# A layer-normalised attention and gate layer: x of batches 1 to 3 arrives with features on partitions, and only token factors are turned

## The chip, the cores and the metric

The kernel runs on one core of one Trainium2 chip. The metric is the device time of one execution in microseconds (us). Beside it stands one profiled execution, whose trace gives every instruction of the five engines: TensorE (PE), VectorE (DVE), ScalarE (ACT), GpSimd (POOL) and SyncE (SP), which here issues nearly all transfers.

## The reference, cut to what matters

For four batches of 512 tokens with 1024 features, in float32:

```
xn = (x - mean(x)) / sqrt(var(x) + 1e-5)          # per token, over features
q, k, v = xn @ Wq.T, xn @ Wk.T, xn @ Wv.T         # 32 query heads, 8 key/value heads, 128 wide
q, k = rmsnorm(q) * q_norm_w, rmsnorm(k) * k_norm_w
attn = softmax(q k^T / sqrt(128) + slope * (key - query), causal)
s = (attn @ v) @ Wo.T
g = silu(xn @ W.T + bias + low-rank part)
out = x + s * g
```

## The kernel before, in words

Every float32 product on TensorE is made of three products of halves: an operand is split into a high part (ACT rounds it) and a low part (the rest, by DVE or POOL), and `three` (L507) multiplies high by high, low by high and high by low.

The work is 32 groups (4 batches by 8 key/value heads), and each group `n` has four steps `j` = 0 to 3, one for each query head of the group. A step is written `(g, j)` here, with `g` the group inside its batch. In every step PE makes the scores of this head and the weighted values of the head before, turns some rows, then makes the projections of the **next** group in two or four "pieces" (`unit_pieces`; 12 products of 448 columns each), then four output products c = 0 to 3 of the head two steps back, with the turning of the probabilities between them. The projection of a group is a 2 x 2 block scheme with seven products P1 to P7: P1, P2 in steps with j = 0, P6, P7 with j = 1, P4 with j = 2, P5, P3 with j = 3. Three of them use blocks of x as they are, four use sums of blocks, made by POOL (`x_sum`).

The engines share no scheduler: the order on each engine is the order in which its block of code issues it (`step` of each engine), and semaphores do the rest. Two PSUM banks hold the pieces and the output products in turn, so output product c = 0 needs the bank of the first piece's row block, c = 1 the second's, c = 2 the bank that DVE frees by adding c = 0 (`add_out`, L1344), and c = 3 the one that it frees by adding c = 1. The turned probabilities use three banks, and the fourth turning needs the first's, which DVE frees (`probs_lo`).

The normalised x of a batch is prepared in the last three groups of the batch before. x lies with tokens on partitions (`xtok`): DVE takes statistics (`ln_stats`, L1241), ACT scales the rows (`ln_scale`, L911), PE turns it in 14 "fills" of four 128 x 128 transposes each (`turn_x`, L581) at steps (6, 3), (7, 0) and (7, 1), and for each fill ACT takes the high part out of PSUM (`x_hi`, L858) and DVE the low part (`x_lo`, L1284). A piece of the next batch waits for the fills of its block.

POOL's order in a step: the position bias of the next head (`bias_of`, L1100), the low part of an output weight (`low_b`, L1092), the low part of v when j = 0 (`values_lo`, L1105), then the low parts of two or four weight tiles (`low_product`, L1081), for the pieces of the next step; they run at the end of a step and in the first 7.7 us of the next one.

## Time and profile before

| what | value |
| --- | --- |
| time, median of 3 runs | 2654.61 us (2654.4 to 2656.84) |
| the profiled execution | 2655.72 us, of which the span of its instructions is 2653.9 us |
| PE busy | 2583.1 us, 97% of the span |
| DVE, ACT, POOL busy | 1699.8, 1764.6, 1718.0 us (64, 66, 65%) |
| mean granted TensorE clock | 0.995 of full speed |
| DMA | 414.78 MB, 156 GB/s in the mean |

A busy PE is counted by instructions that overlap, so its share doesn't show small waits. How long a step takes is read from the timeline: from the first score product of a step (128 x 128) to that of the next. The differences between steps of the same `j` are what a batch's preparation costs.

### The profile page before, as it was taken

How to read it: one execution, taken by the hardware profiler on the slowest of the kernel's cores; microseconds unless marked ns; L12 is line 12 of the kernel's file. 1: busy time of each engine (PE TensorE's matmuls, PEld its weight loads, DVE VectorE, ACT ScalarE, POOL GpSimd, SP SyncE). 2: the span in 40 equal slices, each digit the busy share in tenths (PEclk: the TensorE clock that was granted, in tenths of full speed). 3: DMA queues.
4: the chain of work that ended last, by engine and by line, in shares of the span. 5: the costliest groups of instructions: out<-in, count | busy, mean ns of one | idle time of the engine just before them, and what ended most of it. 6: DMA issues, size and time to landing. Idle time of an engine off the chain costs nothing.

```text
span 2653.9 us, 39893 instructions
## 1 busy us (share of the span) xinstructions
PE 2583.1 (97%) x13840; PEld 2288.9 (86%) x13840; DVE 1699.8 (64%) x3533; ACT 1764.6 (66%) x4633; POOL 1718.0 (65%) x839
## 2 busy tenths in 40 slices
PE   6789999999999999999999999999999999999997
PEld 5778888888888888888888888888888888888886
DVE  7565656666766665666667666666666756656656
ACT  4565666767767666667766667666777666667764
POOL 3577887785767565655667756565666766656555
PEclk9899999999999999999999999999999999999999
DMA  7868878875354333433344433433334533333323
GB/s 283 289 219 278 265 261 272 271 258 166 118 171 154 113 106 118 140 112 118 106 137 155 128 119 111 144 106 118 109 104 137 189 106 108 115 116 112 112 78 131
DMA packets 171896, 414.78 MB, mean 156 GB/s; under 512 B 31024, under 2 KB 63920, under 8 KB 170800
## 3 DMA queue, kind: packets, MB, share of 16 engines
q1 hardware_dynamic: 170144, 410.19, 47.1%
q8 instruction: 112, 1.84, 0.3%
q10 hardware_dynamic: 1552, 2.04, 0.2%
q14 instruction: 88, 0.72, 0.1%
HBM read 339.81 MB, written 89.13 MB: 162 GB/s over the span
## 4 chain that ended last, share of the span: by engine, by line
PE 90%; DVE 3%; DMA 2%; POOL 2%; ACT 1%; SPq 1%; issue 0%; ACTq 0%; POOLq 0%; DVEq 0%
PE proj L508 21%; PE proj L510 21%; PE proj L509 21%; PE tr L608 5%; PE tr L588 3%; PE sc L508 3%; PE sc L509 3%; PE sc L510 3%; PE ot L509 3%; PE ot L510 3%; PE ot L508 3%; DMA wu<-xtok 1%; PE tr L581 1%; DMA wl<-wu 1%; POOL wl L1081 1%
## 5 line engine op out<-in xcount | busy, mean ns | idle before, releaser
L1081 POOL TENSOR_TENSOR wl<-wl,wh 128x896 fp32r<-128x896 f32 x428 | 909.1, 2156 | 552.3 <-ACT wh L788 552.2
L508 PE MATMUL proj<-wh,xh 128*128 128x448 f32 x1792 | 670.7, 374 | 7.3 <-ACT raw L827 2.2
L509 PE MATMUL proj<-wl,xh 128*128 128x448 f32 x1792 | 657.9, 367 | 0.0
L510 PE MATMUL proj<-wh,xl 128*128 128x448 f32 x1792 | 657.8, 367 | 0.0
L1092 POOL TENSOR_TENSOR wb_lo<-wb_lo,wb_hi 128x1024 fp32r<-128x1024 f32 x128 | 307.7, 2404 | 303.7 <-ACT wb_hi L822 303.7
L879 ACT ACTIVATE misc<-misc,negmax 128x128 f32<-128x128 f32 (+3 forms) x512 | 286.7, 565 | 266.3 <-DVE negmax L1319 266.1
L508 PE MATMUL proj<-o_hi,wb_hi 128*128 128x512 f32 x1024 | 425.2, 415 | 7.4 <-DVE acc L1344 3.5
L1344 DVE TENSOR_TENSOR acc<-acc,proj 128x512 f32<-128x512 f32 x476 | 324.8, 683 | 149.7 <-PE proj L510 147.8
L858 ACT ACTIVATE pT_hi<-tr 128x512 fp32r<-128x512 f32 (+3 forms) x512 | 197.5, 440 | 325.9 <-PE tr L608 325.9
L510 PE MATMUL proj<-o_hi,wb_lo 128*128 128x512 f32 x1024 | 403.6, 394 | 0.0
L509 PE MATMUL proj<-o_lo,wb_hi 128*128 128x512 f32 x1024 | 401.3, 392 | 0.0
L788 ACT ACTIVATE wh<-wl 128x896 fp32r<-128x896 f32 x428 | 387.9, 965 | 19.7 <-DMA wl<-wu 19.2
L1314 DVE TENSOR_TENSOR raw<-raw,proj 128x448 f32<-128x448 f32 x320 | 197.4, 617 | 301.9 <-PE proj L510 300.1
L508 PEld LDWEIGHTS proj<-wh,xh 128*128 128x128 f32 x1792 | 337.9, 189 | 37.1 <-ACT raw L827 4.9
L510 PEld LDWEIGHTS proj<-wh,xl 128*128 128x128 f32 x1792 | 337.4, 188 | 30.0
L509 PEld LDWEIGHTS proj<-wl,xh 128*128 128x128 f32 x1792 | 338.1, 189 | 27.8
L1319 DVE CUSTOM_DVE_ANT_0 misc<-sc,misc 128x128 f32<-128x128 f32 (+3 forms) x512 | 240.9, 487 | 175.9 <-PE sc L510 174.7
L1284 DVE TENSOR_TENSOR pT_lo<-tr,pT_hi 128x512 fp32r<-128x512 f32 (+3 forms) x512 | 226.6, 484 | 74.7 <-ACT pT_hi L858 74.4
L834 ACT ACTIVATE junk<-raw 128x128 f32<-128x128 f32 x640 | 189.8, 301 | 97.2 <-DVE raw L1314 93.4
L886 ACT ACTIVATE misc<-misc,rs_inv 128x128 f32<-128x128 f32 (+3 forms) x512 | 245.2, 558 | 1.0 <-DVE rs_inv L1325 1.0
L508 PEld LDWEIGHTS proj<-o_hi,wb_hi 128*128 128x128 f32 x1024 | 193.4, 189 | 51.7 <-DVE acc L1344 4.1
L1100 POOL TENSOR_SCALAR misc<-misc,slope 128x512 f32<-128x512 f32 x128 | 233.6, 1825 | 4.1 <-DMA misc<-rel 4.1
(135 smaller groups left out, 4438.1 us busy)
## 6 DMA issues: line engine op xcount, KB each, us to landing
...
wb_lo<-wo_in SPq DMA_DIRECT2D x128, 512.0 KB, 3.3
...
```

The costliest lines, as they stand in the source:

```text
L508: pe.matmul(out, hi_l, hi_r, start=first, stop=False, skip_group_check=onto)
L509: pe.matmul(out, hi_l, lo_r, start=False, stop=False, skip_group_check=onto)
L510: return pe.matmul(out, lo_l, hi_r, start=False, stop=last, skip_group_check=onto)
L788: act.activation(w_slot(wh, w), w_slot(wl, w, True), ACT.Copy).then_inc(w_hi_done, 1)
L879: act.activation(p, p, ACT.Exp, bias=negmax[:, i:i + 1], scale=-1.0, accum_out=rowsum[:, i:i + 1]).then_inc(exp_done, 1)
L886: ins = act.activation(p, p, ACT.Copy, scale=rs_inv[:, i:i + 1])
L1081: pool.tensor_tensor(w_slot(wl, w), w_slot(wl, w, True), w_slot(wh, w), ALU.subtract).then_inc(w_ready, 1)
L1092: pool.tensor_tensor(wb_lo[:, v % 2, :], wb_lo[:, v % 2, :].bitcast(F32), wb_hi[:, v % 2, :], ALU.subtract).then_inc(wb_ready, 1)
L1100: pool.tensor_scalar(bias_sb[:, m % 2, :], rel_sb[:], slope[:, m % H:m % H + 1], None, ALU.mult).then_inc(bias_ready, 1)
L1284: dve.tensor_tensor(dst, bank, hi, ALU.subtract).then_inc(tr_free, 1)
L1319: dve.tensor_tensor_reduce(prob[:, P_AT[i]:P_AT[i] + w], sc_ps[i % 2][:, 0:w], bias_sb[:, m % 2, S - w:S], -1.0, 3e38, ALU.add, ALU.min, n ...
L1344: dve.tensor_tensor(a, a, bank, ALU.add).then_inc(out_free, 1)
```

## The change

For batches 1 to 3 x is loaded into the same place with features on partitions (eight chunks of 128 features, 512 tokens along each row). Its values then need a factor and a shift that vary along the row, the same for every partition. They come from the tokens: each quarter of x with tokens on partitions is loaded a second time into a new buffer `rows` at steps (4, 3), (5, 0), (5, 1), (5, 2) (`load_rows`), DVE takes its statistics (`row_stats`), ACT and DVE form factor and shift at (5, 3), DVE spreads each over 128 columns (`spread_rows`), PE turns the two (`turn_tokens`, eight transposes at step (6, 0)) and DVE copies them back (`take_rows`). DVE multiplies four parts of x by the factor at (6, 1) (`x_mul`), POOL adds the shift (`x_add`) behind its weight tiles of (6, 1) and ahead of those of (6, 2). ACT and DVE then split each of the seven blocks in one instruction each, of 1024 elements per partition, out of SBUF (`x_hi_later`, `x_lo_later`).

The position bias has one buffer in place of two, so POOL makes the next head's bias only when all four score tiles of this head have been read, and the buffer `junk` of ACT's squares is smaller, with a semaphore on every square.

```diff
+    at = {(6, 3): (P1, P2), (7, 0): (P7, P4, None, P6), (7, 1): (None, None, P5, P3)}
+    return [(b + 1, p) if p is not None else None for p in at.get((g, j), ())]
+
+
+def x_tile(n, j):
+
+    b, g = divmod(n, HKV)
+    t = {(4, 3): 0, (5, 0): 1, (5, 1): 2, (5, 2): 3}.get((g, j))
+    return None if t is None or b + 1 == BATCH else (b + 1, t)
+
+
+def x_count(b, p):
+
+    return NP * (b - 1) + [P1, P2, P7, P4, P6, P5, P3].index(p) + 1
...
+            if (n % HKV, j) == (6, 0) and n + HKV < NG:
+                keys += [("r", n // HKV + 1, i) for i in range(2)]
+            keys += [("p", 4 * n + j, k) for k in range(NT)]
...
-        misc = sb("misc", [P, PW + 5 * S])
-        prob, bias_sb = misc[:, 0:PW], misc[:, PW:PW + 2 * S].rearrange("p (a n) -> p a n", a=2)
-        z_buf, e_buf, rel_sb = (misc[:, PW + i * S:PW + i * S + S] for i in (2, 3, 4))
+        misc = sb("misc", [P, PW + 6 * S])
+        prob = misc[:, 0:PW]
+        bias_sb, z_buf, e_buf, rel_sb = (misc[:, PW + i * S:PW + i * S + S] for i in range(4))
+
+        rows = misc[:, PW + 4 * S:PW + 6 * S]
...
+        def x_part(i):
+
+            chunk, at = i % 2 * 4, i // 2 * 256
+            part = flat(xtok).rearrange("p (k n) -> p k n", k=NK)[:, chunk:chunk + 4, at:at + 256]
+            return part, slice(at, at + 256)
...
-                sp.dma_start(xtok[:], x_tok[b - 1]).then_inc(x_in, 16)
+                chunks = xT[b * NK:b * NK + NK].rearrange("k p n -> p k n")
+                sp.dma_start(flat(xtok).rearrange("p (k n) -> p k n", k=NK), chunks).then_inc(x_in, 16)
+
+            def load_rows(b, t):
+
+                if t > 0:
+                    sp.wait_ge(row_stat, NT * (b - 1) + t)
+                elif b > 1:
+                    sp.wait_ge(x_norm, 4 * (b - 1))
+                sp.dma_start(rows, x_tok[b - 1][:, t, :]).then_inc(rows_in, 16)
...
+            def turn_tokens(b, i):
+
+                key = ("r", b, i)
+                pe.wait_ge(row_spread, b)
+                bank = turn_bank(key)
+                for t in range(NT):
+                    at = i * S + t * P
+                    mm = pe.transpose(bank[:, t * P:t * P + P], rows[:, at:at + P], ident_sb[:])
...
-                for u in pieces:
+                for i, u in enumerate(unit_pieces(n, j)):
                     piece(*u)
-                    if fills:
-                        turn_x(fills.pop(0))
+                    if (n % HKV, j) == (6, 0) and n + HKV < NG and i < 2:
+                        turn_tokens(n // HKV + 1, i)
                 if n + 1 == NG and v % 2 == 0:
                     out_first(v)
                 elif v >= 0:
                     out_ready(v)
                     for c in range(2):
                         out_proj(v, c)
-                        if fills:
-                            turn_x(fills.pop(0))
...
+            def x_hi_later(b, p):
+
+                if p in FILL_SUM:
+                    act.wait_ge(sum_ready, 4 * b + FILL_SUM[p])
+                else:
+                    act.wait_ge(x_norm, 4 * (b - 1) + {P1: 1, P2: 2, P4: 4}[p])
+                act.wait_ge(u_done, u_count(HKV * b - 1, p, 1))
+                act.activation(xh[:, p], x_block(p), ACT.Copy).then_inc(x_hi_done, 1)
...
-                if m >= 2:
-                    wait_alone(pool, scored, 4 * m - 4)
-                pool.tensor_scalar(bias_sb[:, m % 2, :], rel_sb[:], slope[:, m % H:m % H + 1], None,
+                if m >= 1:
+                    wait_alone(pool, scored, 4 * m)
+                pool.tensor_scalar(bias_sb[:], rel_sb[:], slope[:, m % H:m % H + 1], None,
...
+            def split_of(b, p, f):
+
+                if b == 0:
+                    pool.wait_ge(tr_done, TR["x", 0, f] + 1)
+                else:
+                    pool.wait_ge(x_ready, x_count(b, p))
+
+            def x_add(b, i):
+
+                part, at = x_part(i)
+                pool.wait_ge(x_mul_done, 4 * (b - 1) + i + 1)
+                pool.wait_ge(row_free, 2 * b)
+                shift = rows[:, S + at.start:S + at.stop].unsqueeze(1).to_broadcast([P, 4, 256])
+                pool.tensor_tensor(part, part, shift, ALU.add).then_inc(x_norm, 1)
...
-                if (g, j) == (6, 3) and next_x is not None and b > 0:
+                if j == 0 and n + 1 < NG:
+                    values_lo(n)
+                if (g, j) == (7, 1) and next_x is not None:
+                    x_sum(next_x, P5)
+                    x_sum(next_x, P3)
+                if (g, j) == (6, 2) and next_x is not None:
+                    x_add(next_x, 2)
+                    x_add(next_x, 3)
+                if (g, j) == (6, 3) and next_x is not None:
                     x_sum(next_x, P7)
                 if (g, j) == (7, 0) and next_x is not None:
                     x_sum(next_x, P6)
-                if j == 0 and n + 1 < NG:
-                    values_lo(n)
-                if (g, j) == (7, 0) and next_x is not None:
-                    x_sum(next_x, P5)
-                    x_sum(next_x, P3)
...
+                if (g, j) == (6, 1) and next_x is not None:
+                    x_add(next_x, 0)
+                    x_add(next_x, 1)
...
+            def spread_rows(b):
+
+                dve.wait_ge(ln_newton, 5 * (b + 1))
+                for i, column in enumerate((rinv_x, shift_x)):
+                    place = rows[:, i * S:i * S + S].rearrange("p (t n) -> p t n", t=NT)
+                    ins = dve.tensor_copy(place, column[:].unsqueeze(2).to_broadcast([P, NT, P]))
+                ins.then_inc(row_spread, 1)
+
+            def take_rows(b, i):
+                dve.wait_ge(tr_done, TR["r", b, i] + 1)
+                dve.tensor_copy(rows[:, i * S:i * S + S], tr_ps[TR["r", b, i] % 3][:]).then_inc(row_free, 1)
+
+            def x_mul(b, i):
+
+                part, at = x_part(i)
+                dve.wait_ge(x_in, 16 * b)
+                dve.wait_ge(row_free, 2 * b - 1)
+                factor = rows[:, at].unsqueeze(1).to_broadcast([P, 4, 256])
+                dve.tensor_tensor(part, part, factor, ALU.mult).then_inc(x_mul_done, 1)
+
+            def x_lo_later(b, p):
+                dve.wait_ge(x_hi_done, x_count(b, p))
+                dve.tensor_tensor(xl[:, p], x_block(p), xh[:, p], ALU.subtract).then_inc(x_ready, 1)
...
+                        x_lo_later(*turned.pop(0))
+                    fill = fills.pop(0) if fills else None
+                    if fill:
+                        turned.append(fill)
+                    if (g, j) == (6, 0) and next_x and i < 2:
+                        take_rows(b + 1, i)
                     if (j, p, t) == (0, P2, 0):
                         gate_sum(n)
-                    if j == 1 and g == ln_group(b + 1) and next_x:
-                        ln_stats(b + 1, (i,))
+                    if (g, j) == (6, 1) and next_x:
+                        x_mul(b + 1, i)
...
-                turned += fills
+                if x_tile(n, j):
+                    row_stats(*x_tile(n, j))
                 if turned:
-                    x_lo(turned.pop(0))
+                    x_lo_later(*turned.pop(0))
                 add_out(v, 0)
-                if turned:
-                    x_lo(turned.pop(0))
                 if j == 2 and more:
                     row_factors(n + 1, 0)
-                if j == 2 and g == ln_group(b + 1) and next_x:
+                if (g, j) == (5, 3) and next_x:
                     ln_factors(b + 1)
+                    spread_rows(b + 1)
                 add_out(v, 1)
-                if turned:
-                    x_lo(turned.pop(0))
                 for k in range(3):
                     probs_lo(m, k)
                 if j == 1:

```

What moves is shown on POOL, where it makes and consumes x. First POOL before, from the weight tiles of step (6, 1) to those of (6, 3), for batch 2; `wl` is the low part of a weight tile, `misc<-misc,slope` the bias, L1115 the block sum for P7.

```order
L1081 TENSOR_TENSOR wl<-wl,wh 128x896 x4
L1100 TENSOR_SCALAR misc<-misc,slope 128x512
L1092 TENSOR_TENSOR wb_lo<-wb_lo,wb_hi 128x1024
L1081 TENSOR_TENSOR wl<-wl,wh 128x896 x2
L1100 TENSOR_SCALAR misc<-misc,slope 128x512
L1092 TENSOR_TENSOR wb_lo<-wb_lo,wb_hi 128x1024
L1115 TENSOR_TENSOR xtok<-xtok 128x2x512
L1081 TENSOR_TENSOR wl<-wl,wh 128x896 x4
```

The same stretch of POOL now, where L1125 is the weight tile, L1144 the bias, L1136 `low_b`, L1190 `x_add` and L1164 the block sum for P7:

```order
L1125 TENSOR_TENSOR wl<-wl,wh 128x896 x4
L1190 TENSOR_TENSOR xtok<-xtok,misc 128x4x256 x2
L1144 TENSOR_SCALAR misc<-misc,slope 128x512
L1136 TENSOR_TENSOR wb_lo<-wb_lo,wb_hi 128x1024
L1190 TENSOR_TENSOR xtok<-xtok,misc 128x4x256 x2
L1125 TENSOR_TENSOR wl<-wl,wh 128x896 x2
L1144 TENSOR_SCALAR misc<-misc,slope 128x512
L1136 TENSOR_TENSOR wb_lo<-wb_lo,wb_hi 128x1024
L1164 TENSOR_TENSOR xtok<-xtok 128x4x256
L1125 TENSOR_TENSOR wl<-wl,wh 128x896 x4
```

Four additions of 1024 elements stand in POOL's row now, two ahead of a bias and two ahead of the weight tiles of P3.

The second place is DVE in step (7, 0), from the scaling of two query heads to the addition of the output products. Before:

```order
L1274 SCALAR_TENSOR_TENSOR raw<-raw,tmp 128x4x128 x2
L1284 TENSOR_TENSOR xl<-tr,xh 128x512 x2
L1348 TENSOR_SCALAR misc<-misc 128x512
L1284 TENSOR_TENSOR xl<-tr,xh 128x512 x2
L1344 TENSOR_TENSOR acc<-acc,proj 128x512
L1284 TENSOR_TENSOR xl<-tr,xh 128x512
L1344 TENSOR_TENSOR acc<-acc,proj 128x512
L1284 TENSOR_TENSOR xl<-tr,xh 128x512
```

And now (L1376 the scaling, L1352 `x_lo_later`, L1450 the gate's sum, L1446 `add_out`):

```order
L1376 SCALAR_TENSOR_TENSOR raw<-raw,tmp 128x4x128 x2
L1352 TENSOR_TENSOR xl<-xtok,xh 128x1024 x2
L1450 TENSOR_SCALAR misc<-misc 128x512
L1352 TENSOR_TENSOR xl<-xtok,xh 128x1024
L1446 TENSOR_TENSOR acc<-acc,proj 128x512 x2
```

Six low parts out of PSUM have become three out of SBUF, of twice the size, and the third of them (block P6) stands ahead of the addition of output product c = 0.

The third place is POOL in step (7, 0) and (7, 1). Before, `low_b`, the sum for P6, `values_lo`, the sums for P5 and P3:

```order
L1092 TENSOR_TENSOR wb_lo<-wb_lo,wb_hi 128x1024
L1119 TENSOR_TENSOR xtok<-xtok 128x2x512
L1105 TENSOR_TENSOR v_lo<-raw,v_hi 128x512
L1123 TENSOR_TENSOR xtok<-xtok 128x2x512
L1126 TENSOR_TENSOR xtok<-xtok 128x2x512
L1081 TENSOR_TENSOR wl<-wl,wh 128x896 x4
L1100 TENSOR_SCALAR misc<-misc,slope 128x512
L1092 TENSOR_TENSOR wb_lo<-wb_lo,wb_hi 128x1024
```

And now (L1149 `values_lo`, L1168 the sum for P6, L1172 and L1175 those for P5 and P3):

```order
L1136 TENSOR_TENSOR wb_lo<-wb_lo,wb_hi 128x1024
L1149 TENSOR_TENSOR v_lo<-raw,v_hi 128x512
L1168 TENSOR_TENSOR xtok<-xtok 128x4x256
L1125 TENSOR_TENSOR wl<-wl,wh 128x896 x4
L1144 TENSOR_SCALAR misc<-misc,slope 128x512
L1136 TENSOR_TENSOR wb_lo<-wb_lo,wb_hi 128x1024
L1172 TENSOR_TENSOR xtok<-xtok 128x4x256
L1175 TENSOR_TENSOR xtok<-xtok 128x4x256
```

The sum for P6 has moved behind `values_lo`, and those for P5 and P3 to the step after.

## Rows read from the trace of the kernel before

**Rows 1.** The page: the chain that ended last, share of the span by engine.

```profile
PE 90%; DVE 3%; DMA 2%; POOL 2%; ACT 1%; SPq 1%; issue 0%; ACTq 0%; POOLq 0%; DVEq 0%
```

**Rows 2.** Timeline, PE: start us, us; the first score product of a step.

```profile
582.68 0.22 PE L508 MATMUL sc<-kT_hi,qT_hi 128*128 128x128 f32 x1
...
749.81 0.22 PE L508 MATMUL sc<-kT_hi,qT_hi 128*128 128x128 f32 x1
...
1065.15 0.22 PE L508 MATMUL sc<-kT_hi,qT_hi 128*128 128x128 f32 x1
...
1086.33 0.22 PE L508 MATMUL sc<-kT_hi,qT_hi 128*128 128x128 f32 x1
...
1107.51 0.22 PE L508 MATMUL sc<-kT_hi,qT_hi 128*128 128x128 f32 x1
...
1122.79 0.22 PE L508 MATMUL sc<-kT_hi,qT_hi 128*128 128x128 f32 x1
...
1143.96 0.22 PE L508 MATMUL sc<-kT_hi,qT_hi 128*128 128x128 f32 x1
...
1186.32 0.22 PE L508 MATMUL sc<-kT_hi,qT_hi 128*128 128x128 f32 x1
...
1202.24 0.22 PE L508 MATMUL sc<-kT_hi,qT_hi 128*128 128x128 f32 x1
...
1281.06 0.22 PE L508 MATMUL sc<-kT_hi,qT_hi 128*128 128x128 f32 x1
...
1304.04 0.22 PE L508 MATMUL sc<-kT_hi,qT_hi 128*128 128x128 f32 x1
...
1328.69 0.22 PE L508 MATMUL sc<-kT_hi,qT_hi 128*128 128x128 f32 x1
...
1351.56 0.22 PE L508 MATMUL sc<-kT_hi,qT_hi 128*128 128x128 f32 x1
...
1388.02 0.22 PE L508 MATMUL sc<-kT_hi,qT_hi 128*128 128x128 f32 x1
```

**Rows 3.** Timeline, PE, in step (7, 0) of batch 1: one turning of x.

```profile
1311.16 0.60 PE L581 MATMUL tr<-ident_sb,xtok 128*128 128x128 f32 x4
...
1311.51 0.45 PE L508 MATMUL proj<-wh,xh 128*128 128x448 f32 x1
```

**Rows 4.** Timeline, DVE and POOL, at the start of a step with j = 3.

```profile
1124.18 2.89 DVE L1274 SCALAR_TENSOR_TENSOR raw<-raw,tmp 128x512 f32<-128x512 f32 x2
...
1121.72 4.20 POOL L1081 TENSOR_TENSOR wl<-wl,wh 128x896 fp32r<-128x896 f32 x2 [2.55 <-ACT wh L788]
...
1125.90 2.53 POOL L1100 TENSOR_SCALAR misc<-misc,slope 128x512 f32<-128x512 f32 x1
```

**Rows 5.** Groups by form: xcount | busy us, mean ns | idle before, releaser.

```profile
L1092 POOL TENSOR_TENSOR wb_lo<-wb_lo,wb_hi 128x1024 fp32r<-128x1024 f32 x128 | 307.7, 2404 | 303.7 <-ACT wb_hi L822 303.7
...
L1241 DVE BATCH_NORM_STATS2 bn<-xtok 128x6 f32<-128x512 f32 x32 | 20.5, 682 | 7.1 <-DMA xtok<-x_first 7.1
...
L1274 DVE SCALAR_TENSOR_TENSOR raw<-raw,tmp 128x512 f32<-128x512 f32 x160 | 154.6, 998 | 1.1
...
L822 ACT ACTIVATE wb_hi<-wb_lo 128x1024 fp32r<-128x1024 f32 x128 | 134.6, 1052 | 9.5 <-DMA wb_lo<-wo_in 9.5
...
L1366 DVE TENSOR_TENSOR xtok<-xtok,acc 128x512 f32<-128x512 f32 x28 | 38.4, 1372 | 0.1
...
L1284 DVE TENSOR_TENSOR xl<-tr,xh 128x512 fp32r<-128x512 f32 x56 | 37.8, 683 | 18.7 <-ACT xh L858 18.4
...
L1392 DVE TENSOR_TENSOR acc<-acc 128x896 f32<-128x896 f32 x2 | 2.2, 1083 | 0.0
```

**Rows 6.** Timeline, POOL, PE and DVE, late in step (4, 0) of batch 1.

```profile
1079.40 1.29 POOL L1105 TENSOR_TENSOR v_lo<-raw,v_hi 128x512 fp32r<-128x512 f32 x1
...
1083.38 0.48 PE L508 MATMUL proj<-o_hi,wb_hi 128*128 128x512 f32 x1
...
1081.31 0.69 DVE L1344 TENSOR_TENSOR acc<-acc,proj 128x512 f32<-128x512 f32 x1 [1.41 <-PE proj L510]
```

More of the change, by code:

```diff
@@ L110 @@
 TR = {key: i for i, key in enumerate(TURNS)}
-LO = {key: i for i, key in enumerate(k for k in TURNS if k[0] != "z")}
+LO = {key: i for i, key in enumerate(k for k in TURNS if k[0] not in "zr")}
 PROJS = proj_order()
@@ L1244, in ln_stats, with row_stats, ln_variance @@
                 ins.then_inc(ln_stat, 1)
-                wait_alone(dve, ln_stat, 2 * b + 1)
+                wait_alone(dve, ln_stat, 1)
+                ln_variance(0)
+            def row_stats(b, t):
+                dve.wait_ge(rows_in, 16 * (NT * (b - 1) + t + 1))
+                for i in range(2):
+                    ins = dve.bn_stats(bn[:, t, 6 * i:6 * i + 6], rows[:, 512 * i:512 * i + 512])
+                ins.then_inc(row_stat, 1)
+                if t == NT - 1:
+                    wait_alone(dve, row_stat, NT * b)
+                    ln_variance(b)
+            def ln_variance(b):
                 for t in range(NT):
```

124 lines of the change are left out of this document (59 added, 65 removed).

## The prediction

> **What bounds the kernel now.** I read the page first: by the table above PE is busy for 97% of the span, and the chain that ended last lies on PE for 90% [rows 1]. So a microsecond of PE work taken out is a microsecond won, and a microsecond for which PE is made to wait is one lost; the work of the other engines counts only where it makes PE wait. Then I read the lengths of the steps. A group without preparation takes 21.18, 21.18, 15.28 and 21.17 us, 78.81 in all (1065.15 to 1143.96 [rows 2]). Groups 5, 6 and 7 of batch 1, in which batch 2 is prepared, take 1388.02 - 1143.96 = 244.06, that is 7.63 more than three such groups. It lies in (5, 2) with 15.92 (+0.64), (6, 3) with 22.98 (+1.81), (7, 0) with 24.65 (+3.47) and (7, 1) with 22.87 (+1.69). Groups 6 and 7 of batch 0 take 749.81 - 582.68 = 167.13, 9.51 more than two [rows 2]. The third preparation I take as equal to the second. All that can be won is 9.5 + 7.6 + 7.6 = 24.7 us, 0.9%. Last I read the timeline of DVE, ACT and POOL in these steps, to see where each stands when PE needs it.
>
> Times like "at 13.3" below are us after the start of a step. Those of engines that the change leaves alone are where the undisturbed group 4 of batch 1 has them.
>
> **What goes.** A fill of four transposes moves the next piece from 1311.16 to 1311.51, and that piece's first product starts its successor 0.29 instead of 0.20 later: 0.35 + 0.09 = 0.44 [rows 3]. 14 of them make 6.2 of the 7.6 us; the rest is waits of the same steps. All 24.7 go.
>
> The Trainium skill gives 390 ns for a 128x128 bf16 transpose on TensorE (VectorE: DVE Perf Modes, The three transpose paths). By that figure the 144 transposes that go (56 - 8 per batch) would be worth 56 us; by rows 3 four follow each other in 0.35 us, so the measurement decides.
>
> **What comes on PE.** Two turnings at (6, 0): 2 x 0.44 = 0.9 per batch.
>
> **The rule for all that comes on DVE and POOL.** At 1124.18 DVE wants two scalings (two SBUF inputs). POOL's weight tile (two inputs) ends at 1121.72 + 4.20 = 1125.92, and the pair takes 2.89 us; the mean over all 160, many undisturbed, is 998 ns [rows 4, 5]. So DVE's first stands until POOL's instruction ends; the second runs beside POOL's bias (one tensor input), which is stretched to 2.53. Where DVE adds the gate product out of SBUF beside POOL's sums, 512 elements take 1372 ns, out of PSUM 683 (L1366 and L1284 in [rows 5]). I take it that a DVE instruction with two SBUF inputs starts only when POOL's running two-input instruction ends, and that POOL's next one is then held by DVE's length. The new `x_mul` and `x_lo_later` have two SBUF inputs; the old low parts read PSUM and never stood.
>
> The Trainium skill says the same (GPSIMD Engine Reference, Specifications): the SBUF interfaces are shared, with contention for DVE instructions with two SBUF inputs. By that rule the trace agrees, and it speaks against this change; without it the sum is the second rival's.
>
> **Durations.** POOL on 1024 elements: 2.40; ACT on 1024: 1.05; DVE on 896 out of SBUF undisturbed: 1.08, so 1.2 for 1024 [rows 5]. The spread copies are not in the trace: between 0.35 (below half of 0.69, if they ran at double rate) and 0.69 each; I take 0.5.
>
> **Step by step, per batch.**
> - (5, 2): the statistics of the last quarter (two of 0.68 (L1241 in [rows 5]), which with the last take before them end at 10.8, then some 0.7, an estimate from five small operations, for means and variance, of which the last stands for POOL's `low_b` till 11.7) stand before c = 0 is added. c = 1 is added some 1.1 late. In the old (5, 2) a delay of 0.9 on that addition cost PE 0.64 [rows 2]: +0.8.
> - (5, 3): five small operations (1.0) and two copies (1.0) between the additions of c = 0 and c = 1, from 17.3 on; the fourth turning of probabilities waits: +1.0 (0.8 to 1.3).
> - (6, 0): +0.9. The copies find DVE free.
> - (6, 1): four `x_mul` of 1.2 between the pieces, one standing until `low_b` ends at 12.0; the last ends at 16.7 where c = 0 comes at 16.2 and has 1.5 us to spare: 0.
> - (6, 2): two `x_add` on POOL from 7.7 to 12.5. DVE's small row factors stand till 12.5 in place of 11.7: c = 1 is late by 0.9: +0.6.
> - (6, 3): POOL runs bias and `low_b` behind them, into (6, 3); `x_add` 2 and 3 come at 0.6. The two scalings (k and q0, at 1.4) now meet both: k until 3.0 + 0.65, q0 until 6.05 + 0.65 = 6.7. It was done at 4.3 (1124.18 + 2.89 - 1122.79 [rows 2, 4]), and PE turns q0 right then: +2.4. Behind it `low_b` runs from 13.3 to 15.7, the low part of P1 gets in at 15.7 to 16.9, the sum for P7 runs to 19.3, the low part of P2 from 19.3 to 20.5, and only then DVE takes the last piece out of PSUM, at 21.1. PE has waited 0.5 for the bank of c = 0, and wants that of c = 1 at 18.9: +2.2. Together 2.4 + 0.5 + 2.2 = 5.1.
> - (7, 0): without any standing: ACT's two high parts between the takes (2 x 1.05) push the high part of the output weight to 12.2 to 13.3, POOL does `low_b` to 15.7, `values_lo` (1.3 [rows 6]) to 17.0, the sum for P6 to 19.4, ACT its high part to 20.5, DVE its low part to 21.7, and then adds c = 0 (normally at 1081.31 - 1065.15 = 16.2) to 22.4. PE wants that bank for c = 2 at 1083.38 - 1065.15 = 18.2 [rows 6]: +4.2. ACT's squares and the high parts of the probabilities queue behind the same high part, and end by 23.5, beside it.
> - (7, 1): sums for P5 and P3 on POOL from 12.0 to 16.9; low part of P5 until 18.1, a reciprocal of 0.95, low part of P3 to 20.2, c = 0 added to 20.9 where 18.2 is wanted: +2.7.
> - (7, 2): DVE comes to the gate product at 23.1 of (7, 1) in a weight tile of POOL and stands until 24.4; with what is behind it the first score tile is read 2 us late: +1.7.
>
> Sum: 0.8 + 1.0 + 0.9 + 0.6 + 5.1 + 4.2 + 2.7 + 1.7 = 17.0, three times 51.0. Less 24.7: +26.3.
>
> **Edits at nothing.** The single bias buffer: in steps with j = 0, 1, 2 POOL reaches the bias at 7.3, after the fourth score tile (4.5); with j = 3 it reaches it at 1125.90 - 1122.79 = 3.1 [rows 4] and now waits until 5.4, and `low_b` behind it starts at 10.6. Without that cover it would be 2.3 us in 32 steps. The square's semaphore asks for the square before the last, which is over; at worst ACT loses 1 us before its row factors, 0.4 on PE in 31 groups, 12 us. ACT's four scalings of 1.2 go; it wasn't waited for. The 12 loads of 512 KB more find queues that are far from full, and land in steps before they are read.
>
> **The sum.** The profiled execution is 2655.72 us with 1.8 outside its span: 2655.7 + 26.3 = 2682.0. It stands 1.1 over the median of the runs, so 2681.
>
> **The rivals.**
> 1. Much of the standing misses: an instruction's start shifts by tenths, DVE slips in ahead of POOL's, and (6, 3) costs 1, (7, 1) 1.6, (7, 2) nothing, while (7, 0) stays: 0.8 + 1.0 + 0.9 + 0.6 + 1.0 + 4.2 + 1.6 = 10.1, three times 30.3, less 24.7: 2655 + 6 = 2660. For it: many of the 160 scalings show no standing. Against: POOL has more than 20 us of new two-input work per batch in just these steps.
> 2. Faster: splits and sums are all hidden between the pieces, as the work of DVE, ACT and POOL (64 to 66%) leaves room. PE then pays (5, 2), (5, 3) and (6, 0), 2.7 per batch, 8.1 - 24.7 = -16.6: 2638. It decides if the low part of P6 in (7, 0) is done before 17.5. Against: the chain from 13.3 on has 8.4 us of work in four links that only follow each other.
> 3. Slower still: POOL doesn't catch up by the pieces that need its weight tiles, each of the two last waits carries 4 us more into the next step, or the squares cost their 12 us: 2700.
>
> **How the numbers follow.** The first way 0.64, rival 1 0.18, rival 2 0.12, rival 3 0.06. The forecast is 2681; its own range is 2668 to 2694. The range of 8 in 10 takes in the lower case partly and leaves out rival 2: 2655 to 2695. A measurement of this kernel tells 0.2% (5.3 us) from no change. Faster by more: 0.12; within: 0.09 (half of rival 1); slower: 0.79.
>
> **What would show it.** In the profile after: (7, 0) takes 25.4 with DVE idle before the low part of P6 (released by ACT, that by POOL); in (6, 3) the two scalings take over 5 us together, and the step over 25; (7, 2) is over 16.5. The steps (6, 3) to (7, 2) take 1351.56 - 1281.06 + 15.28 = 85.8 before [rows 2] and 92.5 by my sum; if they stay under 88, the prediction is wrong, and if the time still comes out above 2668, it is right by accident.

## The result, and the profile after

The changed kernel takes 2692.9 us in the median (2688.3 to 2702.4), the kernel before 2654.8 us: 1.0148 of its time, with a 95% interval of 1.0135 to 1.0162. The forecast was 2681 us (2655 to 2695) and "slower"; the median lies 2 us under the upper bound, and two of the four runs lie above it. A second measurement in another session (e10_changed_again below) gave 2689.3 us, 1.0133 (1.0119 to 1.0147). The profiled execution took 2702.4 us with a span of 2700.6; before, 2655.7 and 2653.9.

First the page, the chain that ended last:

```profile
PE 82%; DVE 6%; POOL 3%; ACT 3%; DMA 2%; issue 2%; SPq 1%; ACTq 0%; POOLq 0%; DVEq 0%
```

PE has lost 8 points of the chain against [rows 1], six of them to DVE, ACT and POOL (DVE now has 6%, 3% before): PE is made to wait. Where, the step starts of batch 1 tell (timeline, PE; start, duration), in the same form as [rows 2]:

```profile
1242.65 0.22 PE L543 MATMUL sc<-kT_hi,qT_hi 128*128 128x128 f32 x1
...
1264.71 0.22 PE L543 MATMUL sc<-kT_hi,qT_hi 128*128 128x128 f32 x1
...
1285.89 0.22 PE L543 MATMUL sc<-kT_hi,qT_hi 128*128 128x128 f32 x1
...
1302.18 0.22 PE L543 MATMUL sc<-kT_hi,qT_hi 128*128 128x128 f32 x1
...
1331.27 0.22 PE L543 MATMUL sc<-kT_hi,qT_hi 128*128 128x128 f32 x1
...
1358.76 0.31 PE L543 MATMUL sc<-kT_hi,qT_hi 128*128 128x128 f32 x1
...
1384.06 0.22 PE L543 MATMUL sc<-kT_hi,qT_hi 128*128 128x128 f32 x1
...
1399.51 0.22 PE L543 MATMUL sc<-kT_hi,qT_hi 128*128 128x128 f32 x1
```

The first three rows are (6, 0), (6, 1) and (6, 2): what the preparation adds there is small. Then (6, 3) takes 1331.27 - 1302.18 = 29.09 us, (7, 0) 27.49, (7, 1) 25.30, (7, 2) 15.45. Those four took 85.8 us before and take 97.3; the forecast's sum for them was 92.5, and its sign of being wrong was a time under 88. Their engines and TensorE's granted clock, step by step (windows; busy us of each engine, PEclk, DMA):

```profile
1302.18:1331.27 29.09, 23.20 (x116) 20.33 (x115) 24.20 (x29) 14.98 (x43) 17.21 (x9) 0.88 0.29 91
1331.27:1358.76 27.49, 23.78 (x115) 20.76 (x114) 13.94 (x29) 20.58 (x47) 18.45 (x10) 0.89 0.28 87
1358.76:1384.06 25.30, 23.11 (x116) 20.34 (x114) 19.14 (x30) 13.34 (x26) 17.95 (x10) 0.92 0.31 94
1384.06:1399.51 15.45, 15.45 (x84) 13.51 (x83) 8.95 (x25) 11.61 (x35) 8.87 (x5) 1.00 0.30 95
sum 97.33, PE 85.55 PEld 74.94 DVE 66.23 ACT 60.51 POOL 62.48; mean PE 21.39 PEld 18.73 DVE 16.56 ACT 15.13 POOL 15.62
```

PE was busy for 23.2 of 29.1 us in (6, 3). Of the 5.9 us without work 5.51 are one wait (timeline, PE, DVE and POOL at the start of (6, 3); start, duration, line, count, in brackets the idle time before and who ended it):

```profile
1311.60 1.97 PE L626 MATMUL tr<-ident_sb,raw 128*128 128x128 f32 x8 [5.51 <-DVE raw L1376]
...
1303.57 8.58 DVE L1376 SCALAR_TENSOR_TENSOR raw<-raw,tmp 128x512 f32<-128x512 f32 x2
...
1302.21 4.73 POOL L1190 TENSOR_TENSOR xtok<-xtok,misc 128x1024 f32<-128x1024 f32 x2
1306.91 4.09 POOL L1125 TENSOR_TENSOR wl<-wl,wh 128x896 fp32r<-128x896 f32 x2
```

This is the place of [rows 4]. There DVE's pair of scalings took 2.89 us; here it takes 8.58. POOL runs two `x_add` (L1190) and two weight tiles (L1125) one behind the other from 1302.21 to 1311.00, and DVE's first scaling, which is listed from 1303.57, ends 0.6 us after the last of them.

By batch, the time of each step over that of an undisturbed group (21.18, 21.18, 15.28, 21.17), us, in batch 1 ("changed" is the first profile, the columns behind it are explained with the experiments):

| step | forecast | changed | changed again | e11 no norm. | e6 | e9 |
|---|---|---|---|---|---|---|
| (5, 2) | 0.8 | 0.4 | 0.4 | 0 | 0 | 0 |
| (5, 3) | 1.0 | 0.5 | 1.0 | 0 | 0 | 0.6 |
| (6, 0) | 0.9 | 0.9 | 0.9 | 0 | 0.7 | 0.9 |
| (6, 2) | 0.6 | 1.0 | 1.0 | 0 | 1.1 | 1.7 |
| (6, 3) | 5.1 | 7.9 | 3.7 | 2.2 | 1.6 | 0.7 |
| (7, 0) | 4.2 | 6.3 | 3.8 | 5.4 | 2.2 | 0.9 |
| (7, 1) and (7, 2) | 4.4 | 4.3 | 4.1 | 3.9 | 2.1 | 1.7 |
| sum | 17.0 | 21.4 | 15.0 | 11.5 | 7.7 | 6.5 |

Batch 2 has 21.2 in the changed kernel. Batch 0 has 31.0, and there the largest part is (5, 3) with 29.85 us. DVE and POOL in that step (timeline, from 577 us):

```profile
578.07 1.58 DVE L1291 TENSOR_TENSOR tmp_x<-rinv_x 128x4 f32<-128x4 f32 x1 [0.30 <-ACT rinv_x L971]
579.68 0.16 DVE L1293 TENSOR_TENSOR tmp_x<-tmp_x,var_x 128x4 f32<-128x4 f32 x1
579.88 1.97 DVE L1295 TENSOR_SCALAR tmp_x<-tmp_x 128x4 f32<-128x4 f32 x1
581.88 1.98 DVE L1297 TENSOR_TENSOR rinv_x<-rinv_x,tmp_x 128x4 f32<-128x4 f32 x1
583.90 1.99 DVE L1299 SCALAR_TENSOR_TENSOR shift_x<-mv,rinv_x 128x4 f32<-128x4 f32 x1
...
575.43 2.12 POOL L1197 TENSOR_TENSOR xtok<-xtok 128x896 f32<-128x896 f32 x1
577.51 2.11 POOL L1199 TENSOR_TENSOR xtok<-xtok 128x896 f32<-128x896 f32 x1
579.70 2.12 POOL L1201 TENSOR_TENSOR xtok<-xtok 128x896 f32<-128x896 f32 x1
581.78 4.09 POOL L1125 TENSOR_TENSOR wl<-wl,wh 128x896 fp32r<-128x896 f32 x2
...
587.94 0.47 PE L656 MATMUL tr<-ident_sb,misc 128*128 128x128 f32 x1 [7.17 <-DVE pT_lo L1386]
```

Five operations on four elements per partition, of 0.16 to 0.17 us each in batches 1 and 2, take 7.8 us. Four of them end just after an instruction of POOL: two after sums of weight tiles (L1199 and L1201, of `weight_sums`), two after the low parts of weight tiles (L1125) that these sums push back. The four sums stand in (5, 3) in batch 0 alone. The fourth turning of probabilities waits 7.17 us.

### The profile page after: what moved, and what is told of

The parts are those of the page before. It is cut to its first block, busy times and chain, and to the rows that moved or that the text cites. A ratio compares the mean times of both kernels' runs of the same rounds, so it can differ in the third digit from the quotient of the medians.

```text
span 2700.6 us, 39613 instructions
## 1 busy us (share of the span) xinstructions
PE 2585.8 (96%) x13696; PEld 2286.4 (85%) x13696; DVE 1752.7 (65%) x3536; ACT 1751.2 (65%) x4600; POOL 1717.9 (64%) x851
## 4 chain that ended last, share of the span: by engine, by line
PE 82%; DVE 6%; POOL 3%; ACT 3%; DMA 2%; issue 2%; SPq 1%; ACTq 0%; POOLq 0%; DVEq 0%
PE proj L543 19%; PE proj L545 19%; PE proj L544 19%; PE tr L656 4%; PE sc L543 3%; PE sc L544 3%; PE sc L545 3%; PE tr L626 3%; PE ot L544 3%; PE ot L545 3%; PE ot L543 3%; DVE xl L1352 1%; POOL wl L1125 1%; DMA wu<-xtok 1%; DVE acc L1446 1%
## 5 line engine op out<-in xcount | busy, mean ns | idle before, releaser
L1125 POOL TENSOR_TENSOR wl<-wl,wh 128x896 fp32r<-128x896 f32 x428 | 908.0, 2151 | 540.8 <-ACT wh L833 540.7
L1136 POOL TENSOR_TENSOR wb_lo<-wb_lo,wb_hi 128x1024 fp32r<-128x1024 f32 x128 | 307.2, 2400 | 269.9 <-ACT wb_hi L867 269.9
L1446 DVE TENSOR_TENSOR acc<-acc,proj 128x512 f32<-128x512 f32 x476 | 324.7, 683 | 150.7 <-PE proj L545 149.0
L1144 POOL TENSOR_SCALAR misc<-misc,slope 128x512 f32<-128x512 f32 x128 | 203.2, 1587 | 108.3 <-DVE negmax L1421 104.0
L543 PEld LDWEIGHTS proj<-o_hi,wb_hi 128*128 128x128 f32 x1024 | 196.6, 192 | 75.6 <-DVE acc L1446 23.7
```

The lines of the kernel that those rows point to most:

```text
L543: pe.matmul(out, hi_l, hi_r, start=first, stop=False, skip_group_check=onto)
L1125: pool.tensor_tensor(w_slot(wl, w), w_slot(wl, w, True), w_slot(wh, w), ALU.subtract).then_inc(w_ready, 1)
L1136: pool.tensor_tensor(wb_lo[:, v % 2, :], wb_lo[:, v % 2, :].bitcast(F32), wb_hi[:, v % 2, :], ALU.subtract).then_inc(wb_ready, 1)
L1144: pool.tensor_scalar(bias_sb[:], rel_sb[:], slope[:, m % H:m % H + 1], None, ALU.mult).then_inc(bias_ready, 1)
L1446: dve.tensor_tensor(a, a, bank, ALU.add).then_inc(out_free, 1)
```

## The experiments

Lines of the program: the numbers differ by a few from kernel to kernel; the tiles name the operation.

### e1_bias: the parts priced at nothing

```diff
-bias_sb[:, m % 2, S - w:S]                  # two buffers, POOL a head ahead
+bias_sb[:, 0, S - w:S]                      # one, POOL waits for scored 4m
-squares(...): one semaphore for two or three squares
+one for each square
```

> The kernel before with two parts of the change alone: one bias buffer in place of two (POOL's bias of a step waits for the four score reductions of the step before), and ACT's squares counted one by one. The forecast priced both at nothing, so its theory says 2655 +- 2 us. The rival: part of the 38 us that the change cost is a bias that comes late in all 128 steps; 0.1 us for each step would be 13 us, so 2668 us.

Measured: 2654.3 us, ratio 0.9997 (0.9988 to 1.0007). Both parts cost nothing; the rival falls.

### e2_adds: POOL's additions out of its backlog

```diff
-                if (g, j) == (6, 2): x_add(next_x, 2); x_add(next_x, 3)    # behind low_b
+                if (g, j) == (6, 3): x_add(next_x, 2); x_add(next_x, 3)    # ahead of low_b
```

> The changed kernel with POOL's additions 2 and 3 of x moved from step (6,2) to step (6,3), behind the bias, where POOL stands idle from 8.8 to 11.3 and from 12.8 to 16.3 us. Nothing else moves. Theory A (DVE's scaling of the keys waits until POOL has run through its whole backlog, 2 additions and 2 low parts, to 8.8 us of (6,3)): without the additions the backlog ends near 4.2 us, the keys are scaled 4.6 us sooner, (6,3) falls from 29.1 to 24.5 us, three times, with about 1 us each of TensorE's clock: 2677 us. Theory B (the late splits of P1 and P2, which wait for POOL's low part and sum, set the end of (6,3) whatever the keys do): (6,3) falls by at most 1 us, 2690 us. Slower than 2693 only if the additions in (6,3) push the sum P7 and the split P7 beyond what (7,0) can hide.

Measured: 2684.2 us, ratio 1.0106 (1.0091 to 1.0121). (6, 3) fell to 23.8, 23.8 and 23.7 us: theory A's step, a little more than it asked for. In two of the three steps POOL went on ahead of the scaling (3.39 us for it), the case that takes 29.1 us in the changed kernel. Theory B falls. The total fell by less than A said, by 8.8 us against the first measurement of the changed kernel and by 5.2 against the second, since (7, 0) stayed long with 26.6, and steps of batch 0 ahead of the edit, as (5, 0), rose by 1.3.

### e3_sums: the block sums ahead of the low part

```diff
+                if (g, j) == (6, 3): x_sum(next_x, P7)
+                if (g, j) == (7, 0): x_sum(next_x, P6)
+                if (g, j) == (7, 1): x_sum(next_x, P5); x_sum(next_x, P3)
                 low_b(v + 1)
                 values_lo(n)                                           # j == 0
-                (the same four sums here)
```

> The changed kernel with POOL's four sums of x for the next batch moved ahead of its low part of the output weights in the same step: P7 in (6,3), P6 in (7,0), P5 and P3 in (7,1). Theory A (the splits of P6, P5 and P3 stand in a chain behind POOL: low part, values' low part, sum, ACT's split, DVE's split, then the addition that frees TensorE's bank): in (7,0) the sum P6 ends near 13.8 instead of 19.0 us and the first addition of the output goes from 21.3 to about 17.5 us, in (7,1) it goes from 20.0 to about 17.5 us, and P2's split in (6,3) loses its 1.7 us of waiting. (7,0) 27.5 to 23.5, (7,1) 25.3 to 22.5, (6,3) 29.1 to 27.5 us, three times 8.4 us: 2668 us. Theory B (the steps are long because TensorE runs at half its clock there, set off by the wait in (6,3)): the half-clock stretches stay and at most 2 us of each step go, 2685 us. Rival on the other side: the low part of the output weights comes 2 to 5 us later and the output projection waits for it, 2700 us.

Measured: 2671.4 us, ratio 1.0058 (1.0043 to 1.0073), 21.5 us less than the changed kernel's first measurement and 17.9 less than its second. (7, 0) takes 22.3 us in all three batches, (7, 1) 22.1, (7, 2) 16.4. The chain in (7, 0), in the changed kernel (timeline, POOL, ACT, DVE, PE):

```profile
1344.29 2.41 POOL L1136 TENSOR_TENSOR wb_lo<-wb_lo,wb_hi 128x1024 fp32r<-128x1024 f32 x1 [4.17 <-ACT wb_hi L867]
1346.66 1.29 POOL L1149 TENSOR_TENSOR v_lo<-raw,v_hi 128x512 fp32r<-128x512 f32 x1
1347.90 2.37 POOL L1168 TENSOR_TENSOR xtok<-xtok 128x1024 f32<-128x1024 f32 x1
...
1350.30 1.06 ACT L916 ACTIVATE xh<-xtok 128x1024 fp32r<-128x1024 f32 x1 [3.89 <-POOL xtok L1168]
...
1351.39 1.23 DVE L1352 TENSOR_TENSOR xl<-xtok,xh 128x1024 fp32r<-128x1024 f32 x1 [7.05 <-ACT xh L916]
...
1353.27 0.79 PE L543 MATMUL proj<-o_hi,wb_hi 128*128 128x512 f32 x1 [3.71 <-DVE acc L1446]
```

Each link is released by the one above it: low part of the output weight, of v, sum, ACT's high part after 3.89 us of idleness, DVE's low part after 7.05, the addition, and PE after 3.71. The sum itself could have run at 1342.6, when DVE had finished P7's low part. Theory A holds for (7, 0) and (7, 1): in batches 0 and 2, (7, 0) takes 22.3 us at a granted clock of 1.00 though (6, 3) before it had the long wait, which takes theory B away, and the output projection didn't wait for its later low part. (7, 2), which A left out, rose by 1 us.

(6, 3) came out as 28.3, 24.1 and 28.4 us, though nothing around its start had changed. That is the question of e10_changed_again.

### e4_stats and e5_early: the small operations away from the weight sums

```diff
-    t = {(4, 3): 0, (5, 0): 1, (5, 1): 2, (5, 2): 3}.get((g, j))
+    t = {(4, 2): 0, (4, 3): 1, (5, 0): 2, (5, 1): 3}.get((g, j))
-                if (g, j) == (5, 3): ln_rsqrt(b + 1)        # ACT
+                if (g, j) == (5, 2): ln_rsqrt(b + 1)
e4: ln_factors, spread_rows at (5, 3), behind the first piece
e5: ln_factors at (5, 3) ahead of row_sums_inverse, spread_rows where it stood
```

> The changed kernel with the row statistics one step earlier, (4,2) to (5,1), ACT's logarithm and exponential at the end of (5,2), and DVE's five small operations and the two spread copies in (5,3) between the first two pieces, while POOL runs the bias. Theory A (in batch 0 each of the small operations waits for one of POOL's four weight sums of 2.1 us): (5,3) of batch 0 falls from 29.9 to about 22 us and the two half-clock stretches behind it go, the other batches stay within 0.5 us: 2684 us. Theory B (what is slow is the operations' own place in the step, not POOL): (5,3) of batch 0 keeps more than 4 us of its excess, 2690 us or more.

Measured: 2697.7 us, ratio 1.0156 (1.0137 to 1.0175): no gain. (5, 3) of batch 0 fell to 25.0 us, some way to what A had, but in batches 1 and 2 it rose from 21.7 to 23.4 and 25.0, so neither theory came out. The profile shows the reason (timeline of this kernel, DVE and POOL, (5, 3) of batch 1):

```profile
1223.84 0.42 DVE L1335 COPY misc<-shift_x 128x512 f32<-128x512 f32 x1
1224.18 2.88 DVE L1376 SCALAR_TENSOR_TENSOR raw<-raw,tmp 128x512 f32<-128x512 f32 x1
...
1223.99 2.52 POOL L1136 TENSOR_TENSOR wb_lo<-wb_lo,wb_hi 128x1024 fp32r<-128x1024 f32 x1 [3.46 <-ACT wb_hi L867]
```

The two spread copies end at 1224.26, 0.27 us after `low_b` has started, and q1's scaling, 0.68 us in the median of all 160, stands for 2.88. The wait had been moved, not removed.

> The changed kernel with the row statistics one step earlier, (4,2) to (5,1), as in e4_stats, but the five small operations in (5,3) ahead of the inverse of the row sums (near 4.5 us of the step, where POOL has no two-input work) and the two spread copies at the step's end, where they stood. Theory A (in e4_stats the seven operations moved q1's scaling from 8.6 to 10.8 us, into POOL's low part, and each of the three (5,3) paid for that): (5,3) of batch 0 falls from 29.9 to 22 us, the others stay at 21.7, (5,2) loses 0.4 us: 2684 us, 2679 to 2689 with a toss in (6,3) of 5 us for each batch. Theory B (statistics one step earlier are what costs): (5,3) stays above 23 us in batches 1 and 2, 2693 us.

Measured: 2682.9 us, ratio 1.0102 (1.0088 to 1.0116). (5, 3) takes 22.6, 21.2 and 21.2 us, (5, 2) of batches 1 and 2 15.28. The same five operations here (timeline, DVE, (5, 3) of batch 0):

```profile
570.51 0.15 DVE L1291 TENSOR_TENSOR tmp_x<-rinv_x 128x4 f32<-128x4 f32 x1
570.69 0.16 DVE L1293 TENSOR_TENSOR tmp_x<-tmp_x,var_x 128x4 f32<-128x4 f32 x1
570.89 0.61 DVE L1295 TENSOR_SCALAR tmp_x<-tmp_x 128x4 f32<-128x4 f32 x1
571.53 0.17 DVE L1297 TENSOR_TENSOR rinv_x<-rinv_x,tmp_x 128x4 f32<-128x4 f32 x1
571.73 0.16 DVE L1299 SCALAR_TENSOR_TENSOR shift_x<-mv,rinv_x 128x4 f32<-128x4 f32 x1
```

1.4 us in place of 7.8. Theory A holds for (5, 3): it was the neighbour on POOL. The earlier statistics have a price of their own in batch 0: what its steps (4, 3) to (5, 2) take over the undisturbed ones rises from 2.0 us together to 4.8.

### e10_changed_again: one kernel, two outcomes

> The changed kernel once more, for the outcome of the meeting at 2.4 us of (6,3), where POOL's first addition ends and DVE's scaling of the keys has been waiting for 1 us. Theory A (which of the two goes first is open each time and costs 4.2 us, with the low clock behind it up to 5): the profiled run shows for each batch either 29.1 or 24.9 us, nothing between, the runs lie 2680 to 2702 us apart by this, and the median is 2690. Theory B (the program's code decides it): 29.1 us three times, as in the first profile.

Measured: 2689.3 us (2688.6 to 2694.8). (6, 3) takes 24.88, 24.86 and 24.87 us, in the first profile it took 29.06, 29.09 and 29.08: the same program, nothing between. DVE and POOL at the same place (timeline, (6, 3) of batch 1, whose start is at 1301.05):

```profile
1302.44 4.37 DVE L1376 SCALAR_TENSOR_TENSOR raw<-raw,tmp 128x512 f32<-128x512 f32 x2
...
1301.08 5.17 POOL L1190 TENSOR_TENSOR xtok<-xtok,misc 128x1024 f32<-128x1024 f32 x2
...
1306.22 4.66 POOL L1125 TENSOR_TENSOR wl<-wl,wh 128x896 fp32r<-128x896 f32 x2
...
1306.86 0.66 PE L626 MATMUL tr<-ident_sb,raw 128*128 128x128 f32 x4 [1.44 <-DVE raw L1376]
```

Up to 2.4 us into the step the rows of DVE and POOL in both profiles agree to 0.03 us. Then POOL's first `x_add` ends, its second is next, and DVE's scaling has been waiting for 1.0 us. In the first profile POOL went on and did not let DVE in before the end of four instructions. Here DVE got in, k was ready at 2.98 of the step, and POOL's second `x_add` took 2.83 in place of 2.37: PE waited 1.44 in place of 5.51. Five profiles have the same instructions around this place (changed, changed again, e3, e4 and e5), 15 steps in all; DVE went first in 8 of them. Theory A holds for the step. That all three batches of one execution fall alike, as they did in these two, e3 and e4 don't confirm. So the gain of an edit is read here from its step, and not from the total, which holds the outcome at (6, 3) too: by that, e4's total of 2697.7 us has POOL first in two batches of three, e5's has DVE first in all three. The Trainium skill (SBUF — State Buffer, Who interferes with whom) says "Issue order, not op shape, decides who blocks." If DVE, which had waited for 1.0 us when POOL's next one was due, counts as issued first, it should get in each time by that rule; the trace agrees in 8 of 15.

The windows of the same four steps show a second thing:

```profile
1301.05:1325.91 24.86, 21.74 (x116) 18.75 (x114) 19.88 (x29) 14.92 (x43) 18.20 (x9) 1.00 0.34 106
1325.91:1350.89 24.98, 21.46 (x116) 18.95 (x114) 13.77 (x29) 18.95 (x46) 15.91 (x9) 1.00 0.31 95
1350.89:1374.32 23.43, 21.45 (x115) 18.95 (x114) 17.62 (x30) 14.34 (x28) 19.23 (x10) 1.00 0.33 101
1374.32:1391.47 17.15, 15.57 (x84) 13.52 (x82) 10.78 (x26) 12.01 (x35) 10.52 (x6) 1.00 0.28 86
sum 90.42, PE 80.23 PEld 70.16 DVE 62.05 ACT 60.23 POOL 63.86; mean PE 20.06 PEld 17.54 DVE 15.51 ACT 15.06 POOL 15.97
```

(7, 0) takes 24.98 us at a granted clock of 1.00 and took 27.49 at 0.89; 24.98 is near the 25.4 of the forecast's sum of waits. TensorE's clock had fallen to its lower level, 1.2 GHz, in or behind the 5.51 us and the 3.71 us in which it did nothing. Over all steps the changed kernel's first profile has 72 us at that level, this one 38, before 20. Batch 1 is the exception here, not the rule: in batches 0 and 2 of the same profile (7, 0) takes 26.56 and 26.34 us.

```profile
679.01:705.57 26.56, 22.85 (x115) 20.05 (x114) 13.95 (x29) 20.17 (x47) 17.51 (x10) 0.94 0.34 109
1971.47:1997.81 26.34, 22.83 (x116) 19.90 (x114) 13.91 (x29) 20.31 (x47) 17.29 (x10) 0.94 0.29 90
```

The six profiles in which the sum for P6 stands late (changed, changed again, e2, e4, e5 and e11) have 18 such steps: one at a clock of 1.00 with 24.98 us, twelve at 0.94 with 26.3 to 26.6, five at 0.88 to 0.89 with 27.5. PE waits about as long in batch 1 of this profile (3.52 us), where the clock stays up, as in batch 2 (3.51), where it falls; what decides between the two these rows don't show.

In (7, 1) and (7, 2) together the clock made hardly a difference: 40.75 us at 0.92 and 1.00, 40.58 at 1.00. At the lower clock PE reaches (7, 2) later; at the full one it is there sooner and waits 1.58 us for DVE to read the score tile.

### e11_no_norm: what the late splits cost alone

```diff
-ln_rsqrt, ln_factors, spread_rows, turn_tokens, take_rows, x_mul, x_add, load_rows for batches 1 to 3
-act.wait_ge(x_norm, ...)
+act.wait_ge(x_in, 16 * b)
```

> The changed kernel without the normalisation of x for batches 1 to 3 (no row loads, statistics, small operations, turning of the factors, multiplications and additions); the raw x is split and summed in the places of the changed kernel. Theory A (by the step lengths of the changed kernel): (5,2) 0.4, (5,3) 0.5 and in batch 0 8.7, (6,0) 0.9, (6,2) 1.0 go, and of (6,3) what stands over the 22 to 23 us that the late splits and the sum make, about 6.5: 9.3 for each batch and 9 in batch 0, 37 us: 2656 us. Theory B (the forecast's shares, normalisation 3.3 us before (6,3) and 2 in it, the late splits and sums the rest): 16 us, 2677 us.

Measured: 2664.6 us, ratio 1.0036 (1.0022 to 1.0049), between the two, nearer to A. By its steps the splits and sums cost 11.5 us per batch (table above), 34.6 in three, less 24.7 removed: +9.9, and measured is +8.8. So taking the turning out of PE could not have paid even without a normalisation, with the splits and sums placed as they were. These 11.5 us hold the clock of (7, 0) too (26.5 us at 0.94 in all three batches).

### e6_pool, e7_gate, e8_before_gate, e9_spread: POOL's work spread out

```diff
e6 = e3_sums + e5_early, and on POOL
+                if (g, j) == (6, 1):                      # behind low_b
+                    pool.wait_ge(x_mul_done, 4 * next_x)
+                    x_add(next_x, 0); x_add(next_x, 1)
+                if (g, j) == (6, 3):                      # ahead of low_b
+                    x_add(next_x, 2); x_sum(next_x, P7); x_add(next_x, 3)
e7 = e6, gate_product of group 7 behind the fourth gate_inverse
e8 = before, with e7's move of gate_product alone
e9 = e7, x_add 0 in (6, 1), 1 in (6, 2) behind the bias, 2 in (6, 3) ahead of the sum,
     3 in (6, 3) behind low_b; gate_product of the other groups behind the first piece of (n, 1);
     DVE's low part of P6 in (7, 0) behind the addition of c = 1
```

> The changed kernel with three moves together: the sums ahead of the low part (e3_sums), the early small operations (e5_early), and POOL's additions spread out: 0 and 1 in (6,1) behind the low part once all four multiplications are done, 2 and 3 in (6,3) around the sum P7. Theory A (the change's cost lies in where POOL's two-input work stands, not in how much there is): excess over the normal step by batch (5,3) 0.5, (6,0) 0.9, (6,2) 0.5, (6,3) 1.5, (7,0) 1.1, (7,1) 1.0, (7,2) 1.1, together 6.6 us, three times 20 us, against 24.7 us removed: 2650 us, a little faster than before (2655). Theory B (the preparation's own work is too much for POOL and DVE in these steps wherever it stands): at least 12 us for each batch, 2666 us or more. Theory C (TensorE's low clock, set off by any of the remaining waits, keeps half of the excess): 2660 us.

Measured: 2659.1 us, ratio 1.0019 (1.0010 to 1.0027). None of the three theories has it right. The excess by batch is 7.7 us, near A's 6.6, and the profiled run's clock is 0.996, before 0.995, which takes C away although its number, 2660 us, is met. What A left out is batch 0, where the statistics, one step earlier, run into weight sums: its excess is over 5 us more than that of the others.

> e6_pool with the last group's gate product of each batch moved from behind the turned probabilities of (7,1) to behind the fourth gate inverse. Theory A (this product has two inputs and waits for POOL's low part of the weights, 1.7 us, and the third addition of the output behind it): (7,1) loses 0.9 us and (7,2) 0.9 us, three times: 2645 us, 5 below e6_pool. Theory B (the wait has its cover in TensorE's own work): same as e6_pool within 1 us.

Measured: 2658.2 us, ratio 1.0012 (1.0003 to 1.0021), theory B within its 1 us: (7, 2) lost its 1.1 us, (7, 1) gained 0.8.

> The kernel before with the same move of the gate product alone, to see which part of e7_gate's gain has nothing to do with the change. Theory A: (7,1) of before has an excess of 1.6 us, and the product is what sets it: 2650 us. Theory B: there (7,1) is set by the 14 turnings, 2655 us.

Measured: 2655.0 us, ratio 1.0001 (0.9992 to 1.0009): theory B. The place of group 7's product means nothing to the kernel before.

> e7_gate with POOL's work spread further: addition 0 alone in (6,1), 1 in (6,2) behind the bias, 2 in (6,3) ahead of the sum P7, 3 in (6,3) behind the low part; the gate product of every group behind the first piece of its (n,1); DVE's split of P6 in (7,0) behind the second addition of the output. Theory A (each of the remaining excesses is a two-input DVE instruction behind one of POOL's, and goes with it): by batch (6,0) 0.7, (6,2) 0.3, (6,3) 1.2, (7,0) 1.2, (7,1) 0.5 us, in batch 0 3.5 us more, together 15 us against 24.7 removed: 2646 us. Theory B (the waits only change places, as from e6_pool to e7_gate): 2657 us, the same as e7_gate.

Measured: 2652.5 us, ratio 0.9985 (0.9976 to 0.9994), 3.2 us below the kernel before in the same session, between theory A's 2646 and B's 2657. This is 0.15%, less than the 0.2% that the forecast set as its bound, but the interval excludes 1. The steps of batch 1 in its profile, against the first windows above:

```profile
1282.71:1304.57 21.86, 21.46 (x115) 18.84 (x114) 16.48 (x29) 15.00 (x43) 15.83 (x7) 1.00 0.40 121
1304.57:1326.66 22.09, 21.41 (x116) 18.84 (x115) 16.69 (x29) 19.81 (x47) 18.11 (x9) 1.00 0.35 108
1326.66:1349.56 22.90, 21.48 (x115) 18.96 (x114) 16.80 (x31) 13.71 (x27) 17.79 (x10) 1.00 0.34 104
1349.56:1364.84 15.28, 15.28 (x83) 13.56 (x82) 8.64 (x23) 12.03 (x35) 10.64 (x6) 1.00 0.31 96
sum 82.13, PE 79.63 PEld 70.21 DVE 58.61 ACT 60.55 POOL 62.37; mean PE 19.91 PEld 17.55 DVE 14.65 ACT 15.14 POOL 15.59
```

82.1 us in place of 97.3, and 85.8 before. POOL is busy for 62.5 us of these four steps in the changed kernel and for 62.4 here, and it runs 851 instructions in each of the two executions; they stand elsewhere. By the steps of groups 4 to 7 the preparation costs 6.5 and 5.9 us in batches 1 and 2 and 11.3 in batch 0, 23.7 against 24.7 removed: 1.0 us. That is a third of what was measured. The largest other part by the profiles, 2.0 us, lies in the first two groups of batch 0, where the two profiles of the changed kernel differ from each other by 2.6. The gate product of groups 1 to 6 was moved too, and no run has the kernel before with that move. So it is shown that the change, placed well, costs about what it removes; that it gains is not shown.

## Why the prediction was right, and where not

**What goes, 24.7 us.** It was not measured alone, but e11_no_norm's balance (34.6 - 24.7 = 9.9 against 8.8 measured) closes within 1.1 us with it.

**What comes, 17.0 us per batch.** Where DVE went ahead of POOL's next instruction, as assumed (changed again), (5, 2) to (7, 2) cost 25.2, 15.0 and 16.0 us in the three batches. Batch 1 with its 15.0 is the one at full clock. There three of the terms are off: (5, 2) 0.4 for 0.8, (6, 2) 1.0 for 0.6, (6, 3) 3.7 for 5.1.

**(7, 0), 4.2.** The chain was right link by link (its low part of the output weight ends at 15.4 of the step where the forecast had 15.7, DVE's low part at 21.4 for 21.7), and e3_sums removed it: 22.3 us. The forecast was 25.4 us; measured were 24.98 at full clock, once in 18 steps, 26.3 to 26.6 in twelve and 27.5 in five. The clock is a term that the forecast put at nothing, and it is worth 1.4 to 2.5 us in this step.

**(7, 1) 2.7 and (7, 2) 1.7.** Together 4.4, measured 4.3. The sign named for it, (7, 2) over 16.5 us, failed in the first profile (15.45) and came in the second (17.15): the second profile's wait of 1.58 us at the start of (7, 2) is used up in the first by the lower clock at the end of (7, 1). The sum of two steps should have been the sign.

**(6, 3), 5.1.** One step of the argument failed here, the assumption that DVE's instruction "starts only when POOL's running two-input instruction ends, and that POOL's next one is then held by DVE's length". It says who goes first where POOL has the next ready. Measured, this is open each time (8 of 15 as assumed): 24.9 us if DVE does (the forecast had 26.3), 29.1 if POOL does. The sign "the two scalings over 5 us together" came (8.58) in the first profile and not in the second (4.37), though the step was near 25 there too. Three times 4.2 us are about the distance between the spans of the two profiles, 12.7 us. That it is also why all runs of this kernel lie 14 us apart is likely and not shown, as only two of the eight have a profile.

**Batch 0 like the others.** Wrong, and the largest miss of a single step in either profile: (5, 3) costs 8.7 us there and not 1.0. The forecast had a rule that prices most of it (one of the five operations, L1295, has a single input, and stood as long as the others), and that POOL makes weight sums in batch 0's groups 0 to 5 stood in the kernel; it read the undisturbed group of batch 1 for all three. e5_early gives 7.3 of the 8.7 back.

**The edits at nothing** were at nothing (e1_bias).

**The balance.** First profile: 31.0 + 21.4 + 21.2 = 73.6 us come, 24.7 go, +48.9; the spans differ by 46.7, the rest lies in the first two groups of batch 0. The forecast had 51.0. Of the 22.6 between, 7.7 are (5, 3) of batch 0, 8.4 are (6, 3) (three times 7.9 against 5.1) and 6.4 are (7, 0) with its clock. Changed again: 57.9 come, 6.9 over the forecast. Here (5, 3) gives 7.4 and (7, 0) 1.7 more than forecast, (6, 3) gives 4.2 less, and smaller misses of both signs make up the rest.

So the forecast's place and its mechanism, that new work on POOL and DVE makes PE wait in (6, 3) to (7, 2), were right. Its time was 8 to 12 us short, and that it wasn't more is in part luck: batch 0 and the clock, both left out, came on top, and where DVE went first (6, 3) was priced too high. Which of 2689 and 2702 us an execution takes was nothing that the argument could say.

Rival 1, that much of the standing misses, had 2660; only e6_pool and e7_gate, in which the work was placed for that, came there. The condition of rival 2, the low part of P6 done before 17.5 us of (7, 0), came in no run: in e3_sums it ends at 18.7, and in e9_spread it runs from 18.1 to 19.9, behind both additions, and (7, 0) costs 0.9.
